# Feed-forward maxima over pairs of chunks, and ScalarE's taps issued two chunks ahead

## The chip, the cores and the metric

The kernel runs on one core of a Trainium2 chip, as one launch. The metric is the device time of a whole execution in microseconds (us). The core's engines run their own instruction streams in program order and meet at semaphores: TensorE (PE in the profile; its weight loads are PEld), VectorE (DVE), ScalarE (ACT), GpSimd (POOL) and SyncE (SP), which issues DMA transfers.

## The reference

A two-layer block on x of 8 x 512 tokens by 512. Each layer adds a cross-attention and a feed-forward to x, each on a layer-normed x. Layer 1's feed-forward is a mixture of experts; the change lies in layer 0's, a quantized one with a convolution over the sequence:

```python
def act_quant(x):
    scale = 127.0 / jnp.clip(jnp.max(jnp.abs(x), axis=-1, keepdims=True), 1e-05)
    return jnp.clip(jnp.round(x * scale), -128, 127) / scale
def weight_quant(w):
    scale = 1.0 / jnp.clip(jnp.mean(jnp.abs(w)), 1e-05)
    return jnp.clip(jnp.round(w * scale), -1, 1) / scale
def bit_linear(x, w): ...   # quantized x times quantized w
h = bit_linear(x, w1)                                         # 512 -> 2048
h = depthwise_conv1d(h.transpose(0, 2, 1), conv_w, conv_b)    # 3 taps along the sequence
h = h.transpose(0, 2, 1)
h = jax.nn.silu(h)
return bit_linear(h, w2)                                      # 2048 -> 512
```

The second bit_linear needs, for each token, the largest absolute value over all 2048 hidden values before one of them can be rounded.

## The kernel before

The program is a row of stages with barriers between them: projections of the context, attention 0, feed-forward 0 (`ffn`, line 884), attention 1, routing, experts, combination. x stays in SBUF throughout.

`ffn` works batch by batch (B = 8, 512 tokens each), the 2048 hidden values as HC = 16 chunks of 128 partitions by 512 tokens. `iterations` (line 970) calls each engine's `iteration(b, ...)` for b = 0 to 8. In iteration b the engines do three things at once: the middle of batch b (first product, convolution, silu into `hidden`), the back of batch b-1 (scale `hidden` up, round it, second product, sum into x), and the front of batch b+1 (normalize, quantize, transpose). Iteration 0 has no back, iteration 7 no front, iteration 8 only a back. The iterations 2 to 5 are a loop on the device that does two in a turn.

A chunk j of the middle goes through the engines so:

- TensorE `first` (L1064), four matmuls into `product`.
- VectorE `scale_down` (L1261) writes it to `padded`, two chunks ahead of the left tap.
- ScalarE `taps` writes the middle tap to y (L1168) and the right tap to `side` (L1170). y and `side` are `f_shared` in the profile. `padded`, y and `side` have BUF = 4 places.
- VectorE adds the left tap (L1293), GpSimd adds `side` (L1015), ScalarE `silu` (L1182) writes `hidden`.

A chunk j of the back: GpSimd `scale_up` (L1004) multiplies `hidden` by the row `up2_row` (`f_up_row` in the profile), ScalarE `round_up` (L1187), TensorE `second` (L1085). silu(j) of the new batch overwrites what second(j) of the old one has read.

The token maxima are made by `largest(g)` (line 1271): a VectorE reduction over the chunks of group g (L1278), whose elements for one token lie 2048 bytes apart, and from the second group on a maximum with the earlier result (L1282, "join" below). Behind the last one TensorE transposes the maxima (L1107), VectorE reduces them and makes the scales (L1322 to L1327), TensorE spreads them over all partitions (L1112), and ScalarE copies the row to `up2_row` (L1216). Only then can GpSimd begin with the back of this batch. VectorE adds the old batch's product to x (L1310, L1313) in between, and then goes on with the next batch.

What sets the order is the order of the code of each engine and nothing else; there is no planner. TensorE issues first(j+2) and then second(j-1); VectorE scale_down(j+2), left tap j, a `largest` where one is due, and at j = 3 the quantization scales of the next batch (`scales`, L1244 to L1249); GpSimd scale_up(j+2) and right tap j.

Of the kernel before, what the change touches and what calls it, by code (L numbers as in the profile page):

```python
# [56 lines left out]
def at_least(engine, sem, value):  # L57

    if not (isinstance(value, int) and value <= 0):
        engine.wait_ge(sem, value)  # L60
# [823 lines left out]
def ffn(nc, core, w, hidden, w1_in):  # L884
# [11 lines left out]
    HID = 4 * D  # L896
    HC = HID // P
    BUF = 4
    GROUPS = ((0, 5), (5, 10), (10, 14), (14, HC))
    FULL = 127.0  # L900
    SMALLEST = 1e-5
    def low_halves(a):
# [4 lines left out]
    with ExitStack() as stack:  # L907
# [211 lines left out]
        def _(act):  # L1119
# [51 lines left out]
                                     scale=conv_w[:, j % HC, 2:3]).then_inc(taps_made, 1)  # L1171

            taps(0, 0)

            def iteration(b, parity, has_middle, has_back, has_front):
                done = b - 1

                def silu(j):
                    act.wait_ge(right_added, HC * b + j + 1)
                    if has_back:  # L1180
                        act.wait_ge(hq_used, HC * done + j + 1)
                    nc.scalar.activation(hidden[:, j, :], y[:, j % BUF, :], ACT.Silu).then_inc(hidden_made, 1)  # L1182

                def round_up(j):
                    if has_back:
                        act.wait_ge(scaled_up, HC * done + j + 1)
                        nc.scalar.activation(hidden[:, j, :], hidden[:, j, :], ACT.Identity, bias=whole[:, :]  # L1187
                                             ).then_inc(rounded, 1)

                if not has_middle:  # L1190
                    for j in range(HC):
                        round_up(j)
                if has_middle:
                    for j in range(HC):
                        if j + 1 < HC or has_front:
                            taps(b, j + 1)
                        round_up(j)
                        if j > 0:
                            silu(j - 1)
                        if has_front:  # L1200
                            if j in (0, 1):
                                normed(b + 1, 2 * j)
                                normed(b + 1, 2 * j + 1)
                            elif j in (4, 5):
                                to_whole(b + 1, 2 * j - 8)
                                to_whole(b + 1, 2 * j - 7)
                            elif j == 8:
                                copy_row(b + 1, 1 - parity)
                            elif j in (9, 12):
                                copy_front(b + 1, j // 12, 1 - parity)  # L1210
                    silu(HC - 1)

                if has_middle:
                    act.wait_ge(row2_ready, b + 1)
                    at_least(act, scaled_up, HC * b)
                    nc.scalar.activation(up2_row[:, :], scales_bank[:, :], ACT.Copy).then_inc(row2_copied, 1)  # L1216
# [3 lines left out]
        def _(dve):  # L1220
# [47 lines left out]
            def iteration(b, parity, has_middle, has_back, has_front):  # L1268
                done = b - 1

                def largest(g):

                    lo, hi = GROUPS[g]
                    chain = Chain(dve, group_steps, (2 * len(GROUPS) - 2) * b + max(2 * g - 1, 0))
                    at_least(dve, tops_flipped, b)
# [8 lines left out]
                for j in range(HC):  # L1284
# [6 lines left out]
                    if has_middle:  # L1291
# [1 line left out]
                        nc.vector.scalar_tensor_tensor(y[:, j % BUF, :], padded[:, j % BUF, 0:S],  # L1293
                                                       conv_w[:, j, 0:1], y[:, j % BUF, :], ALU.mult, ALU.add
                                                       ).then_inc(left_added, 1)
                    for g in range(len(GROUPS) - 2):
                        if has_middle and j == GROUPS[g][1] + 2:
                            largest(g)
                    if has_front and j == 3:
                        scales(b + 1)  # L1300
                if has_middle:
                    largest(len(GROUPS) - 2)
                    largest(len(GROUPS) - 1)

                def add(i):
# [719 lines left out]
```

## Time and profile before

| | |
|---|---|
| median of 3 runs | 3311.36 us (3308.74 to 3317.6) |
| the profiled execution, its own time | 3314.49 us |
| its span in the trace | 3312.7 us |
| mean granted clock of TensorE | 0.893 of full speed |
| TensorE, VectorE, ScalarE, GpSimd busy over the span | 78%, 56%, 36%, 27% |
| `ffn`, VectorE's first to last instruction of its loop | 650.11 to about 1163.5 us |
| the eight copies of `f_up_row` (L1216) | 707.26 to 1135.58 us |

All later times are from the one profiled execution, counted from the start of its span. The shares over the whole span say little here, because the expert stage fills the second half with TensorE work. A timeline row gives start, length, engine, line, operation, output and inputs; in brackets stands how long the engine had been idle and which instruction released it. An instruction of ScalarE or VectorE begins up to 0.1 us before the one ahead has ended, so the distance of two starts is a little less than a length.

### The profile page before, as it was taken

The numbers are of one execution on the slowest core, as the hardware profiler recorded it, in microseconds if no ns is written. First come the engines' busy times: TensorE is split into PE (matmuls) and PEld (weight loads), VectorE is DVE, ScalarE is ACT, GpSimd is POOL, SyncE is SP. The second block draws the span as 40 slices with busy tenths as digits, with TensorE's granted clock in tenths as the row PEclk, the third lists the DMA queues.
The fourth block names the chain that finished last, engine by engine and source line by source line (L and its number), as shares of the span: only waits on it lengthen the run. The fifth ranks groups of instructions, "written<-read, shape, count | busy, mean of one in ns | idle before, by whom it ended". The sixth has DMA issues, their size and how long they took to land. (4 is left out here: it accounts for less than half of the span.)

```text
span 3312.7 us, 44462 instructions
## 1 busy us (share of the span) xinstructions
PE 2574.8 (78%) x14146; PEld 1327.2 (40%) x14147; DVE 1853.1 (56%) x2672; ACT 1203.9 (36%) x1807; POOL 910.4 (27%) x741
## 2 busy tenths in 40 slices
PE   8377777356666658888887509999999999999970
PEld 4244444122232234444444204444444444444430
DVE  4477776789889676676664642223233333332225
ACT  2233333287887655555554421111111111111110
POOL 0010100066776711111111170005055311350017
PEclk9788888678888879999998859999999999999995
DMA  9560000100000020000000361003033211220018
GB/s 217 119 238 8 7 8 5 51 0 1 1 0 0 0 63 9 9 8 8 11 8 14 117 225 42 32 32 108 32 108 103 76 62 50 89 95 32 32 52 274
DMA packets 118043, 194.11 MB, mean 59 GB/s; under 512 B 55264, under 2 KB 55264, under 8 KB 117456
## 3 DMA queue, kind: packets, MB, share of 16 engines
q1 hardware_dynamic: 92607, 102.96, 11.4%
q0 software_dynamic: 25360, 90.21, 8.0%
q8 instruction: 40, 0.66, 0.1%
q14 instruction: 36, 0.29, 0.0%
HBM read 122.65 MB, written 70.48 MB: 58 GB/s over the span
## 5 line engine op out<-in xcount | busy, mean ns | idle before, releaser
L1806 PE MATMUL e_gate_up<-weights,e_x_t 128*128 x3456 | 772.2, 380 | 1.4 <-ACT e_x_t L1860 1.4
L1806 PEld LDWEIGHTS e_gate_up<-weights,e_x_t 128*128 128x128 bf16 x3456 | 332.8, 98 | 377.4 <-issue 5.1
L1893 DVE TENSOR_TENSOR e_mid<-e_gate,e_gate_up 128x512 f32<-128x512 f32 x144 | 98.9, 687 | 645.8 <-ACT e_gate L1866 645.8
L1826 PE MATMUL e_out<-weights,e_mid_t 128*128 x1728 | 384.7, 379 | 1.1 <-DVE e_mid_t L1906 1.1
L1866 ACT ACTIVATE e_gate<-e_gate_up 128x512 f32<-128x512 f32 x144 | 86.0, 597 | 684.6 <-PE e_gate_up L1806 684.6
L559 PE MATMUL a_turn<-a_wo,a_mixed_t 128*128 128x512 bf16 (+1 forms) x1024 | 284.9, 435 | 2.4 <-DVE a_mixed_t L817 1.7
L1826 PEld LDWEIGHTS e_out<-weights,e_mid_t 128*128 128x128 bf16 x1728 | 169.0, 98 | 204.8 <-issue 1.2
L492 POOL TENSOR_TENSOR a_probs<-a_e,a_probs 128x616 bf16<-128x616 f32 x64 | 85.6, 1353 | 516.4 <-ACT a_probs L726 516.4
L1015 POOL TENSOR_TENSOR f_shared<-f_shared 128x512 f32<-128x512 f32 x128 | 181.0, 1415 | 124.4 <-DVE f_shared L1293 124.4
L1085 PE MATMUL f_out<-f_w,hidden 128*128 128x512 f16 x512 | 143.7, 409 | 91.2 <-ACT hidden L1187 90.7
L650 ACT ACTIVATE a_probs_t<-a_flip 77x512 f32<-77x512 f32 (+1 forms) x256 | 192.3, 801 | 53.7 <-PE a_flip L508 53.6
L1004 POOL TENSOR_TENSOR hidden<-hidden,f_up_row 128x512 f32<-128x512 f32 x128 | 178.6, 1406 | 86.5 <-ACT f_up_row L1216 86.5
L1906 DVE COPY e_mid_t<-e_mid_flip 128x1024 bf16<-128x1024 bf16 x144 | 98.9, 687 | 181.8 <-PE e_mid_flip L1816 181.8
L672 ACT ACTIVATE a_e<-a_e 128x616 f32<-128x616 f32 x128 | 91.6, 717 | 269.3 <-DVE a_e L796 200.5
L1756 POOL TENSOR_TENSOR e_token<-e_token 1x1 f32<-1x1 f32 x6 | 1.1, 183 | 658.6 <-PE e_out L1826 658.6
L559 PEld LDWEIGHTS a_turn<-a_wo,a_mixed_t 128*128 128x128 bf16 (+1 forms) x1024 | 123.5, 122 | 145.8 <-issue 57.3
L1064 PE MATMUL f_product<-f_xq_t,f_w 128*128 128x512 bf16 x512 | 152.3, 431 | 29.4 <-DVE f_padded L1261 20.1
L508 PE MATMUL a_flip<-ident,a_e 128*77 128x128 f32 x512 | 93.1, 341 | 97.7 <-ACT a_probs_t L650 54.0
L1872 ACT ACTIVATE e_y_rows<-e_out 128x512 f32<-128x512 f32 x72 | 43.0, 597 | 340.2 <-PE e_out L1826 340.2
L1293 DVE SCALAR_TENSOR_TENSOR f_shared<-f_padded,f_conv_w,f_shared 128x512 f32<-128x512 f32 x128 | 151.9, 1188 | 11.5 <-ACT f_shared L1170 11.1
L1763 POOL TENSOR_TENSOR weights<-raw_weights,weights 128x1024 bf16<-128x1024 f32 x72 | 154.1, 2140 | 6.1
L1938 POOL DMA_INDIRECT o_y<-sorted_y,plan_rows x64 | 68.6, 1072 | 284.0 <-PEq L1924 264.7
(239 smaller groups left out, 4279.8 us busy)
## 6 DMA issues: line engine op xcount, KB each, us to landing
raw_weights<-in_w POOLq DMA_DIRECT2D x72, 512.0 KB, 4.0
sorted_x<-a_zero_row POOLq DMA_DIRECT2D x1, 18432.0 KB, 55.9
e_x_rows<-sorted_x SPq DMA_DIRECT2D x72, 256.0 KB, 2.7
sorted_y<-e_y_rows SPq DMA_DIRECT2D x72, 256.0 KB, 2.0
raw_weights<-in_w SPq DMA_DIRECT2D x24, 512.0 KB, 4.0
x<-in_x SPq DMA_DIRECT2D x4, 2048.0 KB, 21.7
out<-x SPq DMA_DIRECT2D x32, 256.0 KB, 4.1
hidden<-in_w_t SPq DMA_DIRECT2D x1, 4096.0 KB, 14.4
```

What stands on the lines that cost most here:

```text
L559: last = nc.tensor.matmul(turn[i % 2][:, :], mixed_t[:, a, c, i * P:(i + 1) * P], wo[:, d, c, :], start=(c == 0 and a == d == 0), stop=(c ...
L650: nc.scalar.activation(probs_t[0:KEYS, :, QT * q:QT * (q + 1), i * P:(i + 1) * P], typed(flip[q % 2][:, :])[0:KEYS, :].rearrange("p (a h n ...
L1004: nc.gpsimd.tensor_tensor(hidden[:, j, :], hidden[:, j, :], up2_row[:, :], ALU.mult).then_inc(scaled_up, 1)
L1015: nc.gpsimd.tensor_tensor(y[:, j % BUF, :], y[:, j % BUF, :], side[:, j % BUF, :], ALU.add).then_inc(right_added, 1)
L1064: last = nc.tensor.matmul(product[j % 2][:, :], w1[:, k, j % HC * P:(j % HC + 1) * P], xq_t[:, parity, k, :], start=(k == 0), stop=(k == K ...
L1085: last = nc.tensor.matmul(out[i][:, :], hq[:, j, i * P:(i + 1) * P], w2[:, j, :], start=False, stop=(j == HC - 1))
L1293: nc.vector.scalar_tensor_tensor(y[:, j % BUF, :], padded[:, j % BUF, 0:S], conv_w[:, j, 0:1], y[:, j % BUF, :], ALU.mult, ALU.add).then_i ...
L1763: nc.gpsimd.tensor_tensor(parts[1], plan.raw[:, n % 2, :], parts[0], ALU.subtract).then_inc(split, 1)
L1806: last = nc.tensor.matmul(gate_up[half][:, part, :], x_t[:, u, a, k, :], plan.weights13[:, bass.ds(expert % 2, 1), b, k, col:col + 512], s ...
L1826: last = nc.tensor.matmul(out[:, :], mid_t[:, a, j, :], plan.weights2[:, bass.ds(expert % 2, 1), b, j, :], start=(j == 0 and a == b == 0), ...
L1893: nc.vector.tensor_tensor(mid[:, half, :], gate[:, half, :], gate_up[half][:, 1, :], ALU.mult).then_inc(mid_made, 1)
L1906: nc.vector.tensor_copy(mid_t[:, :, half * MC // 2:(half + 1) * MC // 2, :], mid_flip[half][:, :].rearrange("p (a j n) -> p a j n", a=2, j ...
```

## The change

Three things are changed, all in `ffn`. GROUPS becomes eight pairs of chunks instead of groups of 5, 5, 4 and 2. `largest(g)` is issued one chunk behind the end of its pair plus one (j = hi + 1 instead of hi + 2), for all groups but the last inside the loop over chunks. And ScalarE's order for a chunk becomes silu(j-1), round_up(j), taps(j+2) instead of taps(j+1), round_up(j), silu(j-1), with taps(0, 1) issued ahead of the first iteration. Nothing else is computed and no buffer changes.

```diff
--- before.py
+++ after.py
@@ -896,7 +896,7 @@
     HID = 4 * D
     HC = HID // P
     BUF = 4
-    GROUPS = ((0, 5), (5, 10), (10, 14), (14, HC))
+    GROUPS = tuple((lo, lo + 2) for lo in range(0, HC, 2))
     FULL = 127.0
     SMALLEST = 1e-5
     def low_halves(a):
@@ -1171,6 +1171,7 @@
                                      scale=conv_w[:, j % HC, 2:3]).then_inc(taps_made, 1)
 
             taps(0, 0)
+            taps(0, 1)
 
             def iteration(b, parity, has_middle, has_back, has_front):
                 done = b - 1
@@ -1192,11 +1193,11 @@
                         round_up(j)
                 if has_middle:
                     for j in range(HC):
-                        if j + 1 < HC or has_front:
-                            taps(b, j + 1)
-                        round_up(j)
                         if j > 0:
                             silu(j - 1)
+                        round_up(j)
+                        if j + 2 < HC or has_front:
+                            taps(b, j + 2)
                         if has_front:
                             if j in (0, 1):
                                 normed(b + 1, 2 * j)
@@ -1293,13 +1294,12 @@
                         nc.vector.scalar_tensor_tensor(y[:, j % BUF, :], padded[:, j % BUF, 0:S],
                                                        conv_w[:, j, 0:1], y[:, j % BUF, :], ALU.mult, ALU.add
                                                        ).then_inc(left_added, 1)
-                    for g in range(len(GROUPS) - 2):
-                        if has_middle and j == GROUPS[g][1] + 2:
+                    for g in range(len(GROUPS) - 1):
+                        if has_middle and j == GROUPS[g][1] + 1:
                             largest(g)
                     if has_front and j == 3:
                         scales(b + 1)
                 if has_middle:
-                    largest(len(GROUPS) - 2)
                     largest(len(GROUPS) - 1)
 
                 def add(i):
```

VectorE, the end of a middle iteration (batch 1), before: the last rows before the sums into x. L1278 is a reduction of `largest`, L1282 its join.

```order
L1278 TENSOR_REDUCE f_tops<-hidden 128x512
L1282 TENSOR_TENSOR f_tops<-f_tops 128x512
L1261 TENSOR_TENSOR f_padded<-f_product,f_down_row 128x512
L1293 SCALAR_TENSOR_TENSOR f_shared<-f_padded,f_conv_w,f_shared 128x512
L1261 TENSOR_TENSOR f_padded<-f_product,f_down_row 128x512
L1293 SCALAR_TENSOR_TENSOR f_shared<-f_padded,f_conv_w,f_shared 128x512
L1261 TENSOR_TENSOR f_padded<-f_product,f_down_row 128x512
L1293 SCALAR_TENSOR_TENSOR f_shared<-f_padded,f_conv_w,f_shared 128x512
L1278 TENSOR_REDUCE f_tops<-hidden 128x512
L1282 TENSOR_TENSOR f_tops<-f_tops 128x512
L1278 TENSOR_REDUCE f_tops<-hidden 128x512
L1282 TENSOR_TENSOR f_tops<-f_tops 128x512
```

The same place after, where the lines from 1172 on are one higher (L1262 is scale_down, L1294 the left tap, L1279 and L1283 the maxima).

```order
L1262 TENSOR_TENSOR f_padded<-f_product,f_down_row 128x512
L1294 SCALAR_TENSOR_TENSOR f_shared<-f_padded,f_conv_w,f_shared 128x512
L1279 TENSOR_REDUCE f_tops<-hidden 128x512
L1283 TENSOR_TENSOR f_tops<-f_tops 128x512
L1262 TENSOR_TENSOR f_padded<-f_product,f_down_row 128x512
L1294 SCALAR_TENSOR_TENSOR f_shared<-f_padded,f_conv_w,f_shared 128x512
L1262 TENSOR_TENSOR f_padded<-f_product,f_down_row 128x512
L1294 SCALAR_TENSOR_TENSOR f_shared<-f_padded,f_conv_w,f_shared 128x512
L1279 TENSOR_REDUCE f_tops<-hidden 128x512
L1283 TENSOR_TENSOR f_tops<-f_tops 128x512
L1279 TENSOR_REDUCE f_tops<-hidden 128x512
L1283 TENSOR_TENSOR f_tops<-f_tops 128x512
```

Behind the last left tap stood two reductions and two joins, over four chunks and over two, and now stand two of two chunks each. Between left taps there is now a reduction with a join at every second chunk, where before a reduction stood at two places and a join at one.

ScalarE, the end of iteration 1, before: L1168 and L1170 are the taps, L1187 is round_up, L1182 silu.

```order
L1168 ACTIVATE f_shared<-f_padded,f_conv_b,f_conv_w 128x512
L1170 ACTIVATE f_shared<-f_padded,f_conv_w 128x512
L1187 ACTIVATE hidden<-hidden,f_whole 128x512
L1182 ACTIVATE hidden<-f_shared 128x512
L1168 ACTIVATE f_shared<-f_padded,f_conv_b,f_conv_w 128x512
L1170 ACTIVATE f_shared<-f_padded,f_conv_w 128x512
L1187 ACTIVATE hidden<-hidden,f_whole 128x512
L1182 ACTIVATE hidden<-f_shared 128x512 x2
L1216 ACTIVATE f_up_row<-f_scales_bank 128x512
```

And after (L1188 round_up, L1183 silu, L1217 the copy of `f_up_row`):

```order
L1188 ACTIVATE hidden<-hidden,f_whole 128x512
L1168 ACTIVATE f_shared<-f_padded,f_conv_b,f_conv_w 128x512
L1170 ACTIVATE f_shared<-f_padded,f_conv_w 128x512
L1183 ACTIVATE hidden<-f_shared 128x512
L1188 ACTIVATE hidden<-hidden,f_whole 128x512
L1168 ACTIVATE f_shared<-f_padded,f_conv_b,f_conv_w 128x512
L1170 ACTIVATE f_shared<-f_padded,f_conv_w 128x512
L1183 ACTIVATE hidden<-f_shared 128x512
L1217 ACTIVATE f_up_row<-f_scales_bank 128x512
```

The taps of the next batch's second chunk now stand ahead of the last silu; before, its first chunk's stood ahead of the last two silus, with a round_up between.

ScalarE, the start of iteration 1, before, from the last silus of batch 0 (L1126 normalizes the next batch):

```order
L1182 ACTIVATE hidden<-f_shared 128x512 x2
L1216 ACTIVATE f_up_row<-f_scales_bank 128x512
L1168 ACTIVATE f_shared<-f_padded,f_conv_b,f_conv_w 128x512
L1170 ACTIVATE f_shared<-f_padded,f_conv_w 128x512
L1187 ACTIVATE hidden<-hidden,f_whole 128x512
L1126 ACTIVATE f_xn<-x,shift,rstd 128x512 x2
L1168 ACTIVATE f_shared<-f_padded,f_conv_b,f_conv_w 128x512
L1170 ACTIVATE f_shared<-f_padded,f_conv_w 128x512
L1187 ACTIVATE hidden<-hidden,f_whole 128x512
L1182 ACTIVATE hidden<-f_shared 128x512
L1126 ACTIVATE f_xn<-x,shift,rstd 128x512 x2
L1168 ACTIVATE f_shared<-f_padded,f_conv_b,f_conv_w 128x512
```

And after:

```order
L1183 ACTIVATE hidden<-f_shared 128x512
L1217 ACTIVATE f_up_row<-f_scales_bank 128x512
L1188 ACTIVATE hidden<-hidden,f_whole 128x512
L1168 ACTIVATE f_shared<-f_padded,f_conv_b,f_conv_w 128x512
L1170 ACTIVATE f_shared<-f_padded,f_conv_w 128x512
L1126 ACTIVATE f_xn<-x,shift,rstd 128x512 x2
L1183 ACTIVATE hidden<-f_shared 128x512
L1188 ACTIVATE hidden<-hidden,f_whole 128x512
L1168 ACTIVATE f_shared<-f_padded,f_conv_b,f_conv_w 128x512
L1170 ACTIVATE f_shared<-f_padded,f_conv_w 128x512
L1126 ACTIVATE f_xn<-x,shift,rstd 128x512 x2
L1183 ACTIVATE hidden<-f_shared 128x512
```

Behind the copy of `f_up_row` stood taps of chunk 1, a round_up and the normalizing; now the round_up comes first, then the taps of chunk 2, then the normalizing.

## Rows read from the trace of the kernel before

**Rows 1.** Stretches, middle batch: busy us (instructions), granted clock, DMA share.

```profile
831.00:893.00 62.00, 39.06 (x170) 16.68 (x169) 56.50 (x59) 49.74 (x79) 44.49 (x32) 0.89 0.00 1
```

**Rows 2.** ScalarE timeline: start, us long, instruction, idle before and releaser.

```profile
830.96 0.60 ACT L1216 ACTIVATE f_up_row<-f_scales_bank 128x512 f32<-128x512 f32 x1 [9.63 <-PE f_scales_bank L1112]
...
846.60 1.50 ACT L1132 ACTIVATE f_xn<-f_xn,f_whole,f_up 128x512 f32<-128x512 f32 x2
...
851.87 0.80 ACT L1168 ACTIVATE f_shared<-f_padded,f_conv_b,f_conv_w 128x512 f32<-128x512 f32 x1
...
854.32 0.80 ACT L1168 ACTIVATE f_shared<-f_padded,f_conv_b,f_conv_w 128x512 f32<-128x512 f32 x1
...
862.67 1.25 ACT L1146 ACTIVATE f_xq_t<-f_front,f_back 128x512 bf16<-128x512 f16 x2
...
882.30 0.63 ACT L1182 ACTIVATE hidden<-f_shared 128x512 f32<-128x512 f32 x1 [0.72 <-POOL f_shared L1015]
892.56 0.60 ACT L1216 ACTIVATE f_up_row<-f_scales_bank 128x512 f32<-128x512 f32 x1 [9.63 <-PE f_scales_bank L1112]
...
1077.65 0.60 ACT L1216 ACTIVATE f_up_row<-f_scales_bank 128x512 f32<-128x512 f32 x1 [9.52 <-PE f_scales_bank L1112]
```

**Rows 3.** VectorE timeline, same middle batch.

```profile
834.46 0.69 DVE L1261 TENSOR_TENSOR f_padded<-f_product,f_down_row 128x512 f32<-128x512 f32 x1 [0.29 <-DVE f_down L1332]
...
846.28 0.68 DVE L1261 TENSOR_TENSOR f_padded<-f_product,f_down_row 128x512 f32<-128x512 f32 x1
...
870.09 4.64 DVE L1278 TENSOR_REDUCE f_tops<-hidden 128x512 f32<-128x2560 f32 x1
874.76 0.77 DVE L1282 TENSOR_TENSOR f_tops<-f_tops 128x512 f32<-128x512 f32 x1
...
880.83 3.67 DVE L1278 TENSOR_REDUCE f_tops<-hidden 128x512 f32<-128x2048 f32 x1
...
887.13 0.75 DVE L1310 SCALAR_TENSOR_TENSOR x<-f_out,f_down,x 128x512 f32 x1
```

**Rows 4.** Groups of one form: busy us, mean ns, idle before, releaser.

```profile
L1278 DVE TENSOR_REDUCE f_tops<-hidden 128x512 f32<-128x2560 f32 x16 | 74.6, 4662 | 0.0
...
L1278 DVE TENSOR_REDUCE f_tops<-hidden 128x512 f32<-128x2048 f32 x8 | 29.4, 3673 | 0.2 <-ACT hidden L1182 0.2
...
L1282 DVE TENSOR_TENSOR f_tops<-f_tops 128x512 f32<-128x512 f32 x24 | 17.2, 718 | 0.8
...
L1278 DVE TENSOR_REDUCE f_tops<-hidden 128x512 f32<-128x1024 f32 x8 | 9.8, 1231 | 0.3
```

**Rows 5.** Source view of line 1293: shortest, median, longest ns.

```profile
L1293 DVE SCALAR_TENSOR_TENSOR f_shared<-f_padded,f_conv_w,f_shared x128: 737/1168/1773, 652.5 to 1122.0; 128x512 f32<-128x512 f32 x128
```

**Rows 6.** GpSimd timeline, last batch in the loop.

```profile
1088.96 1.27 POOL L1015 TENSOR_TENSOR f_shared<-f_shared 128x512 f32<-128x512 f32 x1
...
1093.10 1.72 POOL L1004 TENSOR_TENSOR hidden<-hidden,f_up_row 128x512 f32<-128x512 f32 x1
...
1096.01 1.73 POOL L1004 TENSOR_TENSOR hidden<-hidden,f_up_row 128x512 f32<-128x512 f32 x1
```

**Rows 7.** GpSimd timeline, middle batch.

```profile
831.63 3.73 POOL L1004 TENSOR_TENSOR hidden<-hidden,f_up_row 128x512 f32<-128x512 f32 x3 [10.97 <-ACT f_up_row L1216]
...
848.12 1.27 POOL L1015 TENSOR_TENSOR f_shared<-f_shared 128x512 f32<-128x512 f32 x1 [0.62 <-DVE f_shared L1293]
...
873.72 1.26 POOL L1004 TENSOR_TENSOR hidden<-hidden,f_up_row 128x512 f32<-128x512 f32 x1
```

**Rows 8.** Waits, 831 to 893: us in total, times, longest.

```profile
POOL f_shared L1015 <- DVE f_shared L1293: 6.1, 6, 2.2
```

**Rows 9.** VectorE timeline, first and last batch.

```profile
661.68 2.28 DVE L1244 TENSOR_REDUCE f_top<-f_xn 128x4 f32<-128x2048 f32 x1
...
1094.82 0.69 DVE L1261 TENSOR_TENSOR f_padded<-f_product,f_down_row 128x512 f32<-128x512 f32 x1 [1.13 <-PE f_product L1064]
...
1130.27 0.74 DVE L1310 SCALAR_TENSOR_TENSOR x<-f_out,f_down,x 128x512 f32<-128x512 f32 x1
```

## The prediction

> **What bounds the kernel now.** I read the stretches first, then the groups of instructions, then the timelines. The diff touches the feed-forward stage alone, 650 to 1163 us of the span. In a middle batch [rows 1] VectorE works 56.5 of 62 us, ScalarE 49.7, GpSimd 44.5 and TensorE 39.1: three engines are near their limit, and none can be judged alone. I count t from the start of the copy of f_up_row that opens a batch's scaled-up half, 830.96 and 892.56 [rows 2]: one batch is 61.60 us.
>
> The reader is to see two regimes. At a batch's end all others wait for VectorE. ScalarE's last silu ends at 882.93 (t 51.97) [rows 2]. VectorE starts its maximum over four chunks at 880.83 and turns to the sums into x at 887.13 (t 56.17) [rows 3]; 5.43 later f_up_row is copied, after 9.63 us idle on ScalarE [rows 2]. Inside the loop the engines pass chunks on: VectorE's left tap (L1293), GpSimd's right tap (L1015), ScalarE's silu, GpSimd's scaling of the batch before (L1004), ScalarE's rounding, TensorE.
>
> The maxima have a price the size does not suggest [rows 4]: 4662 ns over five chunks, 3673 over four, but 1231 over two. Per chunk that is 932, 918 and 616 ns.
>
> **The change: the maxima.** Before, a batch has two fives, a four and a two, 9.32 + 3.67 + 1.23 = 14.2 us, and three joining operations of 0.72 [rows 4], 2.2: together 16.4. After, eight twos are 9.8 and seven joins 5.0: 14.9. Where nothing interferes, that is 1.5 us less a batch. But the place counts. At the end two of the eight pairs are left: 880.83 to 887.13, 6.30 us, becomes 2 x (1.23 + 0.69 + about 0.05) = 3.95. In the loop, where one join was, there are now five.
>
> **What a join costs there.** The two-input L1293 takes 737 ns at best, 1168 in the median and 1773 at most [rows 5]; GpSimd's operations take 1.27 us or 1.72 [rows 6]. The pattern in the timeline: VectorE waits for the end of GpSimd's instruction, works 0.57, and GpSimd's next begins 0.45 late. In the last batch, where GpSimd never rests, two of its instructions take 1096.01 - 1093.10 = 2.91 us a chunk: twice 1.235 and one delay of 0.45 (1.72 against 1.27) [rows 6]. The one join inside the loop took 0.77 [rows 3], to 0.55 after the end of a GpSimd instruction that started at 873.72 [rows 7]: it waited too. So I charge a join beside a busy GpSimd 1.17 on VectorE and 0.45 on GpSimd. Bounds: 0.69 and nothing; 1.77 and 0.45. A reduction beside a busy GpSimd I charge its bare 1.23, as the fives took the same 4.64 or so there [rows 3]; no pair was measured beside a busy GpSimd, so the upper bound is 1.23 + 0.6 and 0.45 on GpSimd, by what L1293 shows.
>
> The Trainium skill (SBUF — State Buffer, section "SBUF: two separate sides") says that VectorE and GpSimd lock a shared pair of ports for a whole instruction, and that a VectorE operation with two SBUF inputs takes it, one input at plain rate does not. By it five joins a batch are new collisions, and the reductions none; the rows on the join and the fives agree. The same page of the Trainium skill (section "Door 1: The DMA port swizzle", on 16-byte cachelines) says that each access in another line pays a penalty. All these reductions step 2048 bytes, so by it a pair would pay per chunk what a five pays, 1.86 us, and eight pairs would be 5 us dearer than I take. The eight measured pairs [rows 4] say 1231 ns.
>
> **ScalarE's order.** A cycle was silu(j-1), taps(j+2), round_up(j+1); it is now silu(j-1), round_up(j), taps(j+2). Nothing is added: a chunk costs 854.32 - 851.87 = 2.45 us [rows 2]. What moves:
> - At the batch's head taps(1) used to fill the time after the copy. Now round_up(0) stands there and waits for the first of GpSimd's three scalings (3.73 for three [rows 7], so t 1.9), to 2.6; then taps(2) waits for VectorE's scale-down, 834.46 + 0.69 [rows 3], t 4.2. The normalizing that filled this gap now stands behind it. With taps(2) 1.4, two pairs of row operations at 1.41 (1.50 long [rows 2], the next begins 0.09 before their end), silu(0), round_up(1) and taps(3), ScalarE finishes step 1 at t 10.9.
> - Steps 2 to 13 are 12 x 2.45 = 29.4, the work for the next batch between them 2 x 1.41 + 0.6 (a copy of one row, as f_up_row's) + 2 x 1.14 (1.25 long) = 5.7 [rows 2], a wait of about 0.3 for the scale-down of chunk 6: step 14 starts at t 46.3.
> - At the end taps(17) stands ahead of silu(15). Two steps and the silu are 5.5, so the last silu ends at t 51.8 if nobody holds ScalarE up.
>
> **VectorE and GpSimd in the loop.** The first pair's maximum is put ahead of the scales of the next batch (L1244) and moves them, and all behind them, by 1.3 us. VectorE's chunk is 0.60 + 1.17 = 1.77, a maximum with join 1.23 + 0.03 + 1.17 + 0.04 = 2.47. From t 16.65 (before: 846.28, t 15.32 [rows 3]) 12 chunks and five maxima are 21.2 + 12.4 = 33.6: the last left tap ends at t 50.2. For GpSimd, the right tap of chunk 4 starts at 848.12, t 17.2 before [rows 7], at 18.4 after and ends at 19.6. Up to right tap 13 there are 18 instructions at 1.235 and 14 VectorE operations in between (nine left taps, five joins) at 0.45: 22.2 + 6.3 = 28.5, t 48.1. Before, it waited 6.1 us for left taps in this batch, 2.2 at the longest [rows 8], most of it behind the fives; that reserve is now spent on the joins.
>
> **The sum.** silu(13) waits for that right tap: t 48.1, not 46.3. Then 5.5: the last silu ends at 53.6 (before 51.97). Last reduction and join 1.98: t 55.6, against 56.17 [rows 3]. The rest to the next f_up_row, 5.43, is unchanged. So a middle batch (1 to 6) wins 0.57 us, six of them 3.4. The tail's gain of 2.3 is nearly all given back by a loop that is later by 1.6.
>
> Batch 0 has no scaling-up, so GpSimd is half empty. Its scales, at 661.68 [rows 9], come later by 1.3; behind them two fives and a join less (9.9), five pairs with joins more (9.9), but each such break spares the left tap behind it 0.64 (1.38 to 0.74, as GpSimd's tap is then done), 3.2 for five against 1.3 for two: -1.9; tail -2.2. Sum -2.8. Batch 7, from 1077.65 [rows 2], has no batch to prepare. GpSimd's right tap 2 starts at 1088.96 [rows 6] and ends at t 12.6; 11 chunks at 2.91 and five joins at 0.45 put the end of right tap 13 at 46.9. The silus of 13 to 15 then follow GpSimd's taps, 50.5, and the last maximum ends at 52.4, against 1130.27 [rows 9], t 52.6: -0.2, bounds -2.2 (no join delays GpSimd) and +1.4 (each left tap is delayed as well). The stretch behind it, 16 scalings on GpSimd, does not change.
>
> All: -3.4 - 2.8 - 0.2 = -6.4 us. The profiled execution took 3314.49 (span 3312.7 and 1.8 around it), so 3308.1; it lies 3.1 above the median of the three runs, 3311.36, against which I forecast 3305.
>
> **Rivals.**
> 1. *ScalarE alone ends the loop.* If GpSimd is not delayed by each join (they fall into its gaps, bound 0), silu(13) starts at 46.3 and the batch wins 2.37: 6 x 2.37 + 2.8 + 1 = 18 us, 3293. For it: in this batch GpSimd still had six waits [rows 8]. Against: in batch 7, with a full queue, every left tap delayed it [rows 6].
> 2. *The collision price is higher: the pair reduction collides too.* Six reductions at 0.45 hold GpSimd 2.7 longer, so silu(13) starts at 50.8 and a batch loses 2.7 - 0.57 = 2.1, six 12.8; batch 7 loses 2.5, batch 0 wins 1: +14, 3325. It decides the sign as soon as a middle batch's GpSimd is over about 1 us later than I have it. For it: only idle measurements of the pair. Against: the fives beside a busy GpSimd took 4.6 to 4.7 as everywhere.
> 3. *The change does nothing.* round_up now follows silu of its neighbour, so TensorE's second product, which waits for it, and the next first product behind it come later; VectorE waits for products (1.13 us before the chunk at 1094.82 of batch 7 [rows 9]). If each middle batch loses a further half microsecond, only batch 0's gain stays: -3, 3308.
>
> **How the numbers follow.** This kernel's measurement tells a change from none at about 0.3%, 10 us. My forecast has 0.45 (-10 to -2), rival 1 0.27, rival 2 0.12, rival 3 0.16. Faster by over 0.3%: rival 1 and the upper end of the forecast, where half the joins miss GpSimd, 0.25 + 0.12 = 0.37. Slower: rival 2 and a little of rival 3, 0.14. The rest, 0.49, is no change. The range reaches down past rival 1 (3291) and up to half of rival 2 (3317).
>
> **What would show it.** In the new profile: pairs of 1.23 in the loop too (1.5 or more, with GpSimd's L1004 slowed beside them, is rival 2); joins of 0.7 to 1.3; ScalarE idle near 3 us at a batch's head; silu(13) waiting for GpSimd (if not, rival 1); 4 us instead of 6.3 from the last left tap's end to the first sum; f_up_row copies 61.0 us apart. Copies at 59 apart, or over 61.6, prove me wrong.

## The result, and the profile after

The changed kernel takes 3321.74 us (3318.27 to 3326.37, 7 runs) against 3311.36 (3308.66 to 3317.6, 7 runs) beside it: ratio 1.0036, 95% interval 1.0027 to 1.0045. It is 10 us slower. I had forecast 6 us faster, and the time lies 5 us above the top of my range.

The profiled execution has a span of 3320.0 us at a granted clock of 0.892. The last `f_up_row` copy moved from 1135.58 to 1144.80, 9.2 us later, so the loss is made up to there, in the feed-forward. ScalarE's timeline: the copy behind batch 0, the two that enclose the batch followed below, and the two that enclose batch 7:

```profile
701.95 0.60 ACT L1217 ACTIVATE f_up_row<-f_scales_bank 128x512 f32<-128x512 f32 x1 [7.21 <-PE f_scales_bank L1112]
...
828.43 0.60 ACT L1217 ACTIVATE f_up_row<-f_scales_bank 128x512 f32<-128x512 f32 x1 [7.43 <-PE f_scales_bank L1112]
...
892.65 0.60 ACT L1217 ACTIVATE f_up_row<-f_scales_bank 128x512 f32<-128x512 f32 x1 [7.43 <-PE f_scales_bank L1112]
...
1083.65 0.60 ACT L1217 ACTIVATE f_up_row<-f_scales_bank 128x512 f32<-128x512 f32 x1 [7.32 <-PE f_scales_bank L1112]
...
1144.80 0.60 ACT L1217 ACTIVATE f_up_row<-f_scales_bank 128x512 f32<-128x512 f32 x1 [7.31 <-PE f_scales_bank L1112]
```

Up to the first copy 5.3 us are won, of which 2.6 lie ahead of the stage (the first scale-down starts at 647.51 instead of 650.11) and 2.7 in batch 0. Nothing ahead of the stage is changed, and in the traces of the sixteen kernels of this document that scale-down starts anywhere from 644.45 to 654.80: the 2.6 are scatter. From it to the last copy the stage takes 497.29 instead of 485.47, 11.8 more. The six middle batches take 381.70 instead of 370.39, 1.9 more each. The last takes 61.15 instead of 57.93. So -5.3 + 11.3 + 3.2 = +9.2. I go through the batch from 828.43 (t = 0), which stands against [rows 1 to 3, 7]. Its stretch as a whole, columns as in [rows 1]:

```profile
828.40:892.70 64.30, 41.15 (x169) 17.66 (x168) 56.89 (x67) 49.47 (x79) 44.70 (x32) 0.85 0.00 1
```

VectorE, ScalarE and GpSimd are busy within 0.4 us as before [rows 1], and the batch is 2.6 longer than its counterpart. A join's 1.73 us below counts as busy, though most of it is waiting. The first delay is at the batch's head, in ScalarE's timeline:

```profile
830.41 0.72 ACT L1188 ACTIVATE hidden<-hidden,f_whole 128x512 f32<-128x512 f32 x1 [1.38 <-POOL hidden L1004]
832.73 0.81 ACT L1168 ACTIVATE f_shared<-f_padded,f_conv_b,f_conv_w 128x512 f32<-128x512 f32 x1 [1.60 <-DVE f_padded L1262]
...
835.47 0.61 ACT L1183 ACTIVATE hidden<-f_shared 128x512 f32<-128x512 f32 x1
835.99 0.71 ACT L1188 ACTIVATE hidden<-hidden,f_whole 128x512 f32<-128x512 f32 x1
```

The two waits of 2.98 us are the ones I had forecast. What I had not followed is the last row: round_up(1) starts at t 7.56, where before it started at t 5.64:

```profile
836.60 0.71 ACT L1187 ACTIVATE hidden<-hidden,f_whole 128x512 f32<-128x512 f32 x1
```

TensorE and VectorE after, at the same moment:

```profile
836.76 1.89 PE L1085 MATMUL f_out<-f_w,hidden 128*128 128x512 f16 x4 [3.05 <-ACT hidden L1188]
838.44 1.55 PE L1064 MATMUL f_product<-f_xq_t,f_w 128*128 128x512 bf16 x4
840.62 1.04 PE L1085 MATMUL f_out<-f_w,hidden 128*128 128x512 f16 x4 [0.63 <-ACT hidden L1188]
```

```profile
840.02 0.69 DVE L1262 TENSOR_TENSOR f_padded<-f_product,f_down_row 128x512 f32<-128x512 f32 x1 [3.08 <-PE f_product L1064]
...
842.24 1.23 DVE L1279 TENSOR_REDUCE f_tops<-hidden 128x512 f32<-128x1024 f32 x1
843.69 2.29 DVE L1245 TENSOR_REDUCE f_top<-f_xn 128x4 f32<-128x2048 f32 x1 [0.23 <-DVE f_tops L1279]
...
846.84 0.69 DVE L1262 TENSOR_TENSOR f_padded<-f_product,f_down_row 128x512 f32<-128x512 f32 x1
```

TensorE stood idle 3.05 us for that rounding; its next four matmuls take 1.89 and the four of the product 1.55. The rows of the kernel before at this place:

```profile
837.37 1.04 PE L1085 MATMUL f_out<-f_w,hidden 128*128 128x512 f16 x4 [1.12 <-ACT hidden L1187]
838.24 1.03 PE L1064 MATMUL f_product<-f_xq_t,f_w 128*128 128x512 bf16 x4
```

The granted clock is 0.58 from 836.70 to 840.00, mostly the level of 1.2 GHz, and 1.00 (2.4 GHz) at this place before:

```profile
836.70:840.00 3.30, 3.23 (x8) 1.04 (x8) 0.25 (x1) 3.30 (x7) 3.30 (x3) 0.58 0.00 0
```

```profile
837.30:839.30 2.00, 1.90 (x8) 0.70 (x8) 2.00 (x3) 2.00 (x5) 2.00 (x2) 1.00 0.00 0
```

So the product ends at t 11.56 instead of 8.31: 1.92 for the rounding, 0.85 and 0.52 for the clock. VectorE waits 3.08 for it. Its scale-down of chunk 6, from which I counted the loop, starts at t 18.4 (846.84); I had 16.65. The product comes 3.1 us later than before, but only 1.7 of them stay: before, VectorE waited 0.6 for the taps of chunk 3 here, and its `scales` took 0.8 longer. The other 1.4 are the pair's maximum, forecast at 1.3.

TensorE falls to the lower clock in the kernel before too, one step later, where VectorE is busy with `scales` and does not wait for it:

```profile
841.33 1.18 PE L1085 MATMUL f_out<-f_w,hidden 128*128 128x512 f16 x4 [2.06 <-ACT hidden L1187]
842.30 1.91 PE L1064 MATMUL f_product<-f_xq_t,f_w 128*128 128x512 bf16 x4
```

Then the loop. VectorE's timeline of one cycle of two chunks, and GpSimd's:

```profile
856.49 1.23 DVE L1279 TENSOR_REDUCE f_tops<-hidden 128x512 f32<-128x1024 f32 x1
857.75 1.73 DVE L1283 TENSOR_TENSOR f_tops<-f_tops 128x512 f32<-128x512 f32 x1
859.70 0.69 DVE L1262 TENSOR_TENSOR f_padded<-f_product,f_down_row 128x512 f32<-128x512 f32 x1 [0.22 <-DVE f_tops L1283]
...
864.25 1.73 DVE L1283 TENSOR_TENSOR f_tops<-f_tops 128x512 f32<-128x512 f32 x1
```

```profile
855.98 1.72 POOL L1004 TENSOR_TENSOR hidden<-hidden,f_up_row 128x512 f32<-128x512 f32 x1
857.66 1.26 POOL L1015 TENSOR_TENSOR f_shared<-f_shared 128x512 f32<-128x512 f32 x1
858.90 1.72 POOL L1004 TENSOR_TENSOR hidden<-hidden,f_up_row 128x512 f32<-128x512 f32 x1
```

The join begins 0.09 after GpSimd's right tap has begun, waits for its whole length and works 0.56 behind it; GpSimd's next takes 1.72. The cycle repeats, 864.25 - 857.75 = 6.50, and so do all thirty joins in the loops of the six middle batches: each takes 1.72 or 1.73 and starts 0.09 to 0.11 behind a right tap. With the 0.22 behind it a join costs VectorE 1.95, where I charged 1.17 and 0.04. The groups of one form, all batches, beside [rows 4]:

```profile
L1279 DVE TENSOR_REDUCE f_tops<-hidden 128x512 f32<-128x1024 f32 x64 | 78.4, 1225 | 10.2 <-ACT hidden L1183 10.2
L1283 DVE TENSOR_TENSOR f_tops<-f_tops 128x512 f32<-128x512 f32 x56 | 76.2, 1360 | 1.9
```

At last the tail of the same batch:

```profile
882.35 1.22 DVE L1279 TENSOR_REDUCE f_tops<-hidden 128x512 f32<-128x1024 f32 x1
...
885.36 1.23 DVE L1279 TENSOR_REDUCE f_tops<-hidden 128x512 f32<-128x1024 f32 x1 [1.03 <-ACT hidden L1183]
...
887.23 0.74 DVE L1310 SCALAR_TENSOR_TENSOR x<-f_out,f_down,x 128x512 f32 x1
```

4.88 us from the last left tap to the first sum, 6.30 before [rows 3]; what VectorE now waits for is the last silu.

### The profile page after: what moved, and what is told of

The parts are those of the page before. It is cut to its first block and busy times, and to the rows that moved or that the text cites. A ratio compares the mean times of both kernels' runs of the same rounds, so it can differ in the third digit from the quotient of the medians.

```text
span 3320.0 us, 44607 instructions
## 1 busy us (share of the span) xinstructions
PE 2583.3 (78%) x14146; PEld 1332.5 (40%) x14147; DVE 1859.2 (56%) x2736; ACT 1204.3 (36%) x1807; POOL 914.8 (28%) x741
## 5 line engine op out<-in xcount | busy, mean ns | idle before, releaser
L1004 POOL TENSOR_TENSOR hidden<-hidden,f_up_row 128x512 f32<-128x512 f32 x128 | 192.8, 1515 | 76.6 <-ACT f_up_row L1217 76.6
L1015 POOL TENSOR_TENSOR f_shared<-f_shared 128x512 f32<-128x512 f32 x128 | 170.4, 1331 | 142.0 <-DVE f_shared L1294 142.0
L1294 DVE SCALAR_TENSOR_TENSOR f_shared<-f_padded,f_conv_w,f_shared 128x512 f32<-128x512 f32 x128 | 140.8, 1101 | 2.0 <-ACT f_shared L1170 1.9
## 6 DMA issues: line engine op xcount, KB each, us to landing
hidden<-in_w_t SPq DMA_DIRECT2D x1, 4096.0 KB, 14.7
```

Source lines behind the costliest of these rows:

```text
L1004: nc.gpsimd.tensor_tensor(hidden[:, j, :], hidden[:, j, :], up2_row[:, :], ALU.mult).then_inc(scaled_up, 1)
L1015: nc.gpsimd.tensor_tensor(y[:, j % BUF, :], y[:, j % BUF, :], side[:, j % BUF, :], ALU.add).then_inc(right_added, 1)
```

## The experiments

Each run is compared with runs of the kernel before on the same chip. These took 3310.66, 3321.03, 3313.22 and 3311.98 us beside the four sets, so ratios are compared and not times; 0.001 is 3.3 us. "Product waits" are VectorE's waits for `f_product` between 640 and 1175 us: 31.2 us before, 32.0 after.

**The two halves.** `order_only` has ScalarE's order of the changed kernel with the old groups; `pairs_only` has the pairs and their places with the old order.

```diff
 order_only, against the changed kernel: GROUPS = ((0, 5), (5, 10), (10, 14), (14, HC)), largest() where it was
 pairs_only, against the kernel before:  GROUPS = tuple((lo, lo + 2) ...), largest() at j == hi + 1
```

> Only ScalarE's order is changed; the groups of 5, 5, 4 and 2 and their places are those of before. Theory A (two causes: round_up a place later starves VectorE of a product at the batch's head, about 1.8 us in each of seven batches; and joins in the loop cost 1.7 us instead of 0.7): the head's bubble is here in full, the joins are not, and the tail's gain is missing: 8 to 14 us slower than before. Theory B (the joins alone): within 3 us of before. The head's wait for the product (near 3 us before the scale_down of chunk 5) should be in the trace by A.

> Only the groups and their places are changed; ScalarE's order is that of before. Theory A: no bubble at the head, joins of 1.7 us stay: 8 to 14 us faster than the changed kernel, so between 3 slower and 3 faster than before. Theory B: as slow as the changed kernel, 8 to 12 us slower than before. Theory C (the order alone): the 2.3 us of the tail are won in full, 12 to 18 us faster than before.

`order_only` took 3340.71 us, ratio 1.0089 [1.0076, 1.0102] (the interval is of 95%); `pairs_only` 3307.70, 0.9988 [0.9979, 0.9997]. The order alone costs 30 us, more than twice what I had expected; the pairs alone win 4. On top of the pairs the order costs 1.0036 - 0.9988, 16 us. In `order_only` the product waits are 72.3 us in 35 waits, and the trace has the same place as above, TensorE and VectorE:

```profile
850.78 1.89 PE L1085 MATMUL f_out<-f_w,hidden 128*128 128x512 f16 x4 [3.04 <-ACT hidden L1188]
852.47 1.85 PE L1064 MATMUL f_product<-f_xq_t,f_w 128*128 128x512 bf16 x4
```

```profile
854.35 0.69 DVE L1262 TENSOR_TENSOR f_padded<-f_product,f_down_row 128x512 f32<-128x512 f32 x1 [3.36 <-PE f_product L1064]
```

In `pairs_only` the product waits are 10.1, so on top of the pairs the order adds 22 us to them. There the loops' joins take 1.71 to 1.74 in the middle batches as well, and in the batch from 824.70 the scale-down of chunk 6 starts at t 16.95, where I had forecast 16.65:

```profile
841.65 0.68 DVE L1261 TENSOR_TENSOR f_padded<-f_product,f_down_row 128x512 f32<-128x512 f32 x1
```

The pairs and the order don't add (30 alone, 16 together). In `order_only` a middle batch is 4.8 us longer than before, and only 1.5 of them are there when chunk 6 is scaled down; the others come with further product waits, in the batch followed 3.41 at t 25.5 and 2.33 at t 39.6 (0.41 and 1.81 before). The changed kernel has 0.56 at t 26.8. Why these later waits go with the groups of 5, 5, 4 and 2 is not shown. That joins keep VectorE back does not explain it alone: with one-input joins (below) the order costs less still, 0.9985 - 0.9950, 12 us.

**Which part of the order.** Two kernels put round_up(j) ahead of silu(j-1) again, with the taps still two ahead.

```diff
+                        round_up(j)
                         if j > 0:
                             silu(j - 1)
-                        round_up(j)
                         if j + 2 < HC or has_front:
                             taps(b, j + 2)
```

> The changed kernel with one swap: round_up(j) ahead of silu(j-1), taps(j+2) still last. Theory A: the bubble at the head goes, as round_up(1) starts two operations of normalizing and a silu earlier or at least the silu earlier; since the normalizing of step 0 still stands ahead of it, only 0.5 of the 1.8 us comes back there: 3 to 5 us faster than the changed kernel. If the place of round_up against silu is what counts all over the loop: 8 to 12 us faster. Theory B: no difference.

> Groups of before, ScalarE's order round_up(j), silu(j-1), taps(j+2): the cycle of three is the same as before, only the work for the next batch stands behind the taps instead of ahead of them. Theory R (the place of round_up behind silu(j-1) is what makes the order-only kernel 30 us slower: TensorE waits 3 us for it, falls to half clock and hands VectorE its product late): nearly all of it comes back, within 5 us of before. Theory S (the taps and normalizing at the batch's head cost it): it stays 15 us or more slower than before.

`round_first` (the changed kernel with this edit) took 3311.05, 1.0002 [0.9993, 1.0011]: 11 of its 16 us are back, where I had expected 3 to 5 from the head alone and 8 to 12 if the place of the rounding counts all over the loop. `order_round_first` (the same on `order_only`) took 3319.88, 1.0019 [1.001, 1.0028]: 23 of 30 are back. TensorE's wait at the head falls to 2.42, and its next four matmuls take 1.04 again, the product 1.68 (`round_first`):

```profile
841.74 1.04 PE L1085 MATMUL f_out<-f_w,hidden 128*128 128x512 f16 x4 [2.42 <-ACT hidden L1188]
842.62 1.68 PE L1064 MATMUL f_product<-f_xq_t,f_w 128*128 128x512 bf16 x4
```

VectorE's wait there is 1.87 instead of 3.08. One ScalarE operation of 0.6 us ahead of the rounding was most of the order's loss. The rest, 5 to 6 us, belongs to the taps two ahead and the normalizing behind them, which no run parts.

**A larger lag on TensorE.** If the product is late only because second(j-1) stands ahead of it, one more chunk of lag should free it.

```diff
 order_only with
-                LAG = 1
+                LAG = 2
```

> The order-only kernel with TensorE's second product one chunk further behind the first (LAG 2). If the order costs time because VectorE waits for a first product that stands behind a second product that waits for round_up: the waits for f_product fall from 72 us to under 40 and the time by 15 to 30 us against the order-only kernel. If it costs through silu, which may only overwrite what the second product has read: those waits (16.5 us) grow and the time is the same or longer.

`order_lag2` took 3353.88, 1.0093 [1.0079, 1.0107]: no gain. The product waits did fall, from 72.3 to 44.7. But silu(j) overwrites what second(j) reads, and ScalarE's waits of silu for `f_out` rose from 16.5 to 51.6:

```profile
ACT hidden L1183 <- PE f_out L1085: 51.6, 28, 3.8
DVE f_padded L1262 <- PE f_product L1064: 44.7, 22, 6.6
```

The loss moved to another wait. A late rounding is paid for with either lag: the product waits behind `second`, or silu waits for it.

**The joins.** `one_input_join` makes the five joins of the loop reductions over two rows of `f_tops`, which has a third row for it: operations with one input.

```diff
-result(nc.vector.tensor_tensor(tops[:, 0, :], tops[:, 0, :], tops[:, 1, :], ALU.max))
+out_row, in_rows = (2, slice(0, 2)) if g % 2 else (0, slice(1, 3))
+result(nc.vector.tensor_reduce(tops[:, out_row, :], tops[:, in_rows, :].rearrange("p a n -> p n a"), AX.X, ALU.max))
```

> The changed kernel, but the five joins inside the loop are done as reductions over two neighbouring rows of tops (one input, so no lock against GpSimd), with a third row for the result. Each takes 1.23 us instead of 1.73 plus 0.22 and should not delay GpSimd by 0.45. Theory A: the two-chunk cycle falls from 6.50 us to between 5.8 and 6.1, so 2 to 3.5 us in each of six batches: 12 to 20 us faster than the changed kernel. Theory C (the head's bubble alone is the loss): within 3 us of it, or slower for the longer operation.

`one_input_join` took 3306.72, 0.9985 [0.9976, 0.9995]: 17 us faster than the changed kernel, though a join of this kind works nearly twice as long as the bare 0.69. VectorE, and GpSimd's instruction behind the join at 848.17:

```profile
846.92 1.22 DVE L1279 TENSOR_REDUCE f_tops<-hidden 128x512 f32<-128x1024 f32 x1
848.17 1.24 DVE L1285 TENSOR_REDUCE f_tops<-f_tops 128x512 f32<-128x1024 f32 x1
849.63 0.69 DVE L1262 TENSOR_TENSOR f_padded<-f_product,f_down_row 128x512 f32<-128x512 f32 x1 [0.22 <-DVE f_tops L1285]
...
852.95 1.23 DVE L1279 TENSOR_REDUCE f_tops<-hidden 128x512 f32<-128x1024 f32 x1
```

```profile
849.31 1.27 POOL L1004 TENSOR_TENSOR hidden<-hidden,f_up_row 128x512 f32<-128x512 f32 x1
```

This join too starts 0.09 behind a right tap (848.08), but it doesn't wait for it, and GpSimd's next takes 1.27 instead of 1.72. The cycle of two chunks is 6.03 us instead of 6.50.

`join_later` keeps the two-input join and puts it behind the next scale-down, off the beat.

```diff
+                    for g in range(1, len(GROUPS) - 2):          # behind scale_down(j + 2)
+                        if has_middle and j == GROUPS[g][1] + 2:
+                            join(g)
```

> The changed kernel, but each of the five joins in the loop stands behind the next scale_down instead of directly behind its reduction. Theory P (the join costs 1.73 us because it starts just as GpSimd has begun an instruction, and would cost less at another moment): started 0.6 us later it takes 1.1 to 1.2, five joins in six batches save 12 to 18 us against the changed kernel. Theory Q (VectorE pays GpSimd's instruction at its next two-input operation anyway): the join is shorter but the left tap behind it waits as long, and the time is within 4 us of the changed kernel.

`join_later` took 3324.98, 1.0006 [0.9998, 1.0015]: 10 us faster than the changed kernel, less than the one-input joins give and between the two expectations. Joins fell from 1360 to 1046 ns in the mean, but the left tap behind them, which also has two inputs, met GpSimd in their place (1.64 us at 856.90), and the cycle there is still 6.48. More than half of what a middle batch wins, 0.7 of 1.15 us, is there before the loop, at the scale-down of chunk 6; why is open.

`no_loop_joins` leaves the joins of the loop out but for one of 512 tokens, so its maxima are not the tokens'.

```diff
+nc.vector.tensor_reduce(tops[:, 0, 0:1], tops[:, 1, 0:2], AX.X, ALU.max)      # in the loop, instead of the join
```

> The changed kernel, where the five joins in the loop work on one of 512 tokens by a one-input operation (so the maxima of most tokens miss ten chunks): semaphores and reductions stay, the joins' length and their lock go. It bounds what joins cost. If VectorE's chain in the loop sets the pace: five times about 1.8 us in each of six batches, 35 us and more faster than the changed kernel. If TensorE's late products or ScalarE set it: 15 to 22 us faster, hardly more than the one-input joins gave.

`no_loop_joins` took 3307.15, 0.9977 [0.9967, 0.9988]: 20 us less than the changed kernel, only 3 less than with one-input joins, although 8 x 5 x 1.24 = 50 us of VectorE's work are gone. The product waits rise to 64.1 us, from 27.4 with one-input joins: in this order VectorE's own work no longer sets the loop's pace, and what is taken from it turns into waits for products.

**Do the two causes add?** `pairs_one_input`: old order, pairs, one-input joins. `rf_one_input`: `round_first` with one-input joins.

> Both repairs: ScalarE's order of before, pairs of chunks, and the joins in the loop as reductions with one input. If the two causes add (the order 14.0 us, the joins 15.0 us against the changed kernel): 3293, 17 us faster than before. If another engine takes over (ScalarE needs 2.45 us a chunk and the work for the next batch, 51.8 us to its last silu by the prediction's count): a middle batch not under 59.2 us, so 3296 to 3302.

> The changed kernel with both repairs, round_up(j) ahead of silu(j-1) and one-input joins in the loop. By the two single repairs (10.7 and 15.0 us) 3296; if what limits it is ScalarE with taps(17) ahead of the last silu, it stays above the kernel that has before's order (0.995 of before): 0.996 to 0.998 of before.

They took 3302.85 and 3302.37 us, ratios 0.9950 [0.9934, 0.9965] and 0.9968 [0.9955, 0.9982]. From 1.0036, undoing the order gives 0.0048 and the joins 0.0051, together 0.0099; measured 0.0086. The rounding's place (0.0034) and the joins give 0.0085; measured 0.0068. They add but for 4 to 6 us, so they are two causes.

**Other groups.** In the old order, `tail_pairs` has 5, 5, 2, 2, 2 and `tail_threes` 3, 3, 3, 3, 2, 2.

> Before, with only the group of four split: groups 5, 5, 2, 2, 2, the last two at the end. VectorE then has one reduction of two and a join more in the loop (1.23 + 0.03 + 0.7 to 1.9) and 2.35 us less behind the last left tap. If the loop has room for it (VectorE waits 4 us a batch there): 1 to 2 us a batch, 8 to 16 us faster than before. If it has none: within 3 us of before.

> Before with groups 3, 3, 3, 3, 2, 2. It measures a reduction over three chunks (by the fours' and fives' 0.93 us a chunk 2.75 us, by the pairs' 0.61 1.83 us). At 2.75 VectorE has 4 x 2.75 + 2 x 1.23 + five joins, more than before, and the tail saves 2.35: 0 to 10 us slower than before. At 1.83 a batch saves 4.4 us of reductions and pays two joins: 5 to 15 us faster.

`tail_pairs` took 3315.75, 0.9981 [0.9973, 0.9990]: the shorter tail with one more join in the loop is worth 6 us, between the two expectations. `tail_threes` took 3290.32, 0.9934 [0.9919, 0.9949], 22 us faster than before, the best ratio of all and more than I had expected. Its groups:

```profile
L1278 DVE TENSOR_REDUCE f_tops<-hidden 128x512 f32<-128x1536 f32 x32 | 61.0, 1907 | 0.0
L1282 DVE TENSOR_TENSOR f_tops<-f_tops 128x512 f32<-128x512 f32 x40 | 35.4, 884 | 1.4
```

A reduction over three chunks takes 1907 ns, 636 a chunk, nearly as cheap as a pair, while the four and the five took 918 and 932 [rows 4]. And there are three joins in the loop, not five, which take 1.05 us. VectorE's join and the GpSimd instruction it meets:

```profile
846.82 1.06 DVE L1282 TENSOR_TENSOR f_tops<-f_tops 128x512 f32<-128x512 f32 x1
```

```profile
846.05 1.27 POOL L1004 TENSOR_TENSOR hidden<-hidden,f_up_row 128x512 f32<-128x512 f32 x1
```

The join starts 0.77 behind GpSimd's instruction, not 0.09, and waits only for the rest of it. The reduction ahead of it is 0.68 us longer than a pair's, and 0.09 + 0.68 is 0.77: the length of the reduction sets where the join meets GpSimd.

**What was still open.** Does the order cost as much on these groups too (`threes_new_order`), and do one-input joins win anything where the two-input ones meet GpSimd later (`threes_one_input`)?

> Groups of three chunks (3,3,3,3,2,2), with ScalarE's order of the changed kernel. Theory that the order costs by itself, by the product that comes late behind the hidden rounding: 14 to 30 us slower than the threes alone, ratio 0.9975 to 1.0025, with product waits of VectorE again over 40 us between 640 and 1175. Theory that the order's cost in the changed kernel came from its meeting with reductions of pairs: within 4 us of the threes alone, ratio 0.9925 to 0.995.

> Groups of three chunks (3,3,3,3,2,2) in the order of the kernel before, and the joins inside the loop done as one-input reductions over three rows of f_tops. The joins in the loop measured 884 ns x40 over all with two inputs. Theory that the joins held VectorE's chain only where they met a GpSimd instruction each time (1.72 us, as in the changed kernel): here they don't, so a one-input join of 1.24 us is no gain: within 4 us of the threes alone, ratio 0.9925 to 0.995. Theory that a two-input join costs beyond its own length whatever its phase (0.22 us behind it and what it delays on GpSimd): 5 to 10 us faster than the threes alone, ratio 0.9905 to 0.992.

`threes_new_order`: 3314.52, 1.0008 [0.9999, 1.0017], 24 us slower than the threes alone, with product waits of 53.1 (21.1 without). The same place again:

```profile
836.99 1.80 PE L1085 MATMUL f_out<-f_w,hidden 128*128 128x512 f16 x4 [3.04 <-ACT hidden L1188]
```

`threes_one_input`: 3287.93, 0.9941 [0.9927, 0.9954], the same as the threes alone. On these groups a one-input join of 1.24 us wins nothing against a two-input one of 1.05; on pairs, against 1.73, it did.

## Why the prediction was wrong

It failed in two terms of the middle batch, which both stood in the text with too low a price. Over the stage, from its first scale-down to the last copy, I had -6.4 and the traces have +11.8. Of the 18.2 us between them 14.7 lie in the six middle batches and 3.4 in batch 7. In the batch shown, the period was 64.22 where I had 61.03:

- *"From t 16.65".* The failed step. I followed ScalarE at the head, its waits of 1.9 to 2.6 and up to 4.2 came out, and then started VectorE as if only the pair's 1.3 us stood in its way. The late round_up(1) goes on to TensorE, which falls to its lower clock, and to the product VectorE needs: t 18.4, 1.75 late (in the mean of the six batches 18.0, 1.35 late). With the old order it is t 16.95 in the batch looked at (mean 16.9). Rival 3 named this chain and priced it at "a further half microsecond"; it was about three times that. The runs with the rounding first, and the order on three groupings (30, 16 and 24 us), show it.
- *"So I charge a join beside a busy GpSimd 1.17".* It was 1.73 and the 0.22 behind it, 1.95, above my upper bound of 1.77. I took the median of the left tap, as if joins met GpSimd at random. They don't: all five start in the same phase. The loop took 35.5 instead of 33.6, 1.9 late. Five joins at 0.74 more are 3.7, and a product wait is 0.6; against them, the twelve left taps took 11.7 where 12 x 1.17 = 14.0 were charged, since one behind a join takes 0.74 to 0.85. The same median was too low for the joins and too high for the left taps. The one-input joins show the joins' price (-17 us).
- *The tail.* 5.4 forecast from the last left tap to the first sum, 4.88 measured: 0.5 won back. 1.75 + 1.9 - 0.5 = 3.2, the miss of this batch.
- *Batch 0.* -2.8 forecast; from its first scale-down to its copy it took 54.44 instead of 57.15, -2.7. Right. Its five loop joins take the bare 0.71 or 0.72, as GpSimd is half empty there.
- *Batch 7.* -0.2 forecast, bounds to +1.4; +3.2 measured. There too the joins take 1.72, and VectorE's last reduction then waits 3.53 for the last silu. That silu waits 2.04 for TensorE's second product of the old batch, whose rounding now stands behind the silu ahead:

```profile
1136.86 0.63 ACT L1183 ACTIVATE hidden<-f_shared 128x512 f32<-128x512 f32 x1 [2.04 <-PE f_out L1085]
1137.62 1.23 DVE L1279 TENSOR_REDUCE f_tops<-hidden 128x512 f32<-128x1024 f32 x1 [3.53 <-ACT hidden L1183]
```

  I had followed only GpSimd's taps here. With the rounding first again (`round_first`) the batch takes 57.92.
- *The pair reductions.* Right: 1225 ns in the mean of 64, in the loop too. Rival 2, which alone was to make the kernel clearly slower, is refuted; that its time, 3325, was near is chance. By the Trainium skill ("SBUF — State Buffer", section "SBUF: two separate sides") a VectorE operation with two SBUF inputs contends with a GpSimd operation that reads SBUF: the one that starts first keeps the other out for its whole length, while a VectorE operation with one SBUF input, outside the modes that use both port pairs, doesn't contend. The traces agree: the joins of the loop take 1.73 with two inputs and 1.24 with one, though both start 0.09 behind a right tap.
- *silu(13) waits for GpSimd at t 48.1.* It starts at t 50.0, 0.04 behind the end of GpSimd's right tap 13, but only 0.1 later than ScalarE's own taps would let it. GpSimd is late because it waited 0.63 for VectorE's left tap of chunk 12. The loop was VectorE's, not GpSimd's.

The text's own mark, "over 61.6" between copies, was met: 63.6 in the mean.

Not separated by a run: how much of the order's cost is the lower clock and how much the plain delay. In the batch followed here they are 1.37 and 1.92 us of 3.3 at the product's end. And `join_later` changed more than where the joins meet GpSimd, so it doesn't bound what that is worth.

## What to carry to other kernels

Where an operation is put behind another of its engine, follow its result to the end, through every engine that waits for it, and not only the engine itself; here an operation of 0.6 us on ScalarE, put ahead of the rounding, was most of the 16 to 30 us that the order cost. A contended instruction in a periodic loop had no average price here: it met the other engine in the same phase each time, so work out the beat and price it by that phase, as the one loop join of the kernel before (0.77, 1.04 behind GpSimd's instruction) and those behind threes and pairs (1.05 and 1.73, at 0.77 and 0.09) show. Measure a strided reduction at each group size before choosing one; here three chunks in a group took nearly the cheap price and four did not.

## What the runs showed of the hardware that was not expected

- For 512 outputs of elements 2048 bytes apart, a VectorE maximum takes 1.23 us over two, 1.91 over three, 3.67 over four and 4.66 over five. The step between three and four is 1.76 us, the others about 0.7 to 1.0.
- Behind a TensorE wait of 3.05 us four matmuls took 1.89 and the next four 1.55, at a granted clock of 0.58; behind one of 2.42 they took 1.04 and 1.68; behind one of 2.06, 1.18 and 1.91; behind one of 1.12, 1.04 and 1.03. The wait just ahead doesn't settle it alone: in `round_first` one of 1.31, shortly behind the 2.42, was followed by 1.89 and 1.91.
- A two-input join on VectorE that starts 0.09 us behind a GpSimd instruction waits for that instruction's whole 1.26 us, and the next GpSimd instruction is 0.45 us longer. The two engines keep this phase: four cycles of 6.50 us in a row, against 6.03 to 6.06 with a one-input operation of 1.24 us, which starts in the same phase.
